# Products without a use of their results in the first steps of an attention, and scale vectors that are loaded later

## The chip, the cores and the metric
One core of a Trainium2 chip runs the whole program. The metric is the time of one execution on the device, in microseconds; the profile gives its span, from the first to the last instruction, and every instruction inside it.

## What is computed
Four blocks, each with a residual sum and a layer normalisation behind it, on 2 x 1024 tokens of 128 features, all in float32:

```
x = LN(x + attention0(x))     # 8 heads of 16, queries and keys; each head's values have 128 columns
x = LN(x + ffn0(x))           # silu(x W1^T * s1) * (x W2^T * s2), then two gelu layers of 512, then back to 128
x = LN(x + attention1(x))     # gated delta rule in chunks of 32, short and long filters
x = LN(x + ffn1(x))           # +1/-1 weights, three layers
```

Attention0, where the change lies, is `softmax((xn Wq + bq)(xn Wk + bk)^T / 4) (xn Wv + bv)` for each of 2 x 8 = 16 heads, and the results are summed over groups of eight. The vectors w1_s, w2_s, h1_s, h2_s (512 numbers each) and w3_s (128) scale the outputs of ffn0's layers.

## The kernel before, in words
The five engines have one program each, and semaphores connect them. The attention is a list of steps written out by hand, `for step in range(LAST + 1)` in the TensorE program. A head is two units of 512 query rows; unit u has four steps. In a step TensorE (PE) does up to four things, for four different stages of the pipeline:

- `scores(u, m)` (line 1629): two products of 50 x 128 by 50 x 512 into a ring of three PSUM banks (4, 5, 6). ScalarE (ACT) turns each into probabilities (line 628, exponential). It lies in step `4(u+1) + 7 + m`.
- `row_scores` (lines 1608, 1609): two products of 48 x 128 by 48 x 512, side by side in the array, into bank pair 0-1 or 2-3. VectorE (DVE) takes the maximum of each row from them (line 1110). Step s needs the maximum of step s - 2 to be taken.
- `shift_to_rows(u)` (line 1617), in step `4(u+1) + 2`: GpSimd (POOL) has split the maxima (lines 803, 804), PE transposes them, ACT copies them (line 622), and the queue of SyncE (SP) sends them by two small DMAs into rows 48 to 49 and 112 to 113 of the query stack (`load_shift`, line 381). `scores(u, 0)` waits for them.
- `pv` (line 1644): 16 products of 128 x 32 by 128 x 128, probabilities times values, into bank 7.

The SP queue is one list in program order. For each head h it has: `load_shift(2h)`, some stores or loads, the stacks of head h + 3 (`load_stacks`, lines 375 and 376, four DMAs of 192 KB, which for h + 3 >= 4 wait until the scores of head h - 1 are done), `load_shift(2h + 1)`, and more stores or loads. Among them, at h = 2, lie the five small loads of the scale vectors (lines 399 and 400), then the weights of ffn0, at h = 7 and 8 the weights of attention1. Steps 1 to 3 also hold the last projections: `project_q(3)`, `project_k(3)`, `project_v(3)`; DVE reads the last of them from bank 7 in `values(3)` (line 1087), behind the maximum of step 4.

ACT and DVE wait for all ffn0 loads, scales and weights together, before ffn0's first silu; POOL waits for them at unit 13, where it begins to split the weights. The scales count in the same semaphore, `w_in`, as the weights.

The names of the diff: `T_BANK[3]` is bank 4, `PVB` bank 7, `MAXB` bank 0; `ksp[0]` and `qsp[0]` hold the split keys and queries of the first 512 tokens and stay unchanged through the attention. `score_step(1, 0)` is step 15, `pv_step(0, 0)` is step 14.

Of the kernel before, what the change touches and what calls it, by code (L numbers as in the profile page):

```python
# [9 lines left out]
P = 128  # L10
# [4 lines left out]
GROUPS = B * S // GT  # L15
# [41 lines left out]
def program(nc, dr, out_dram, x_dram, q_scratch, k_scratch, ctx):  # L57
# [3 lines left out]
    def sem(name):  # L61
        return ctx.enter_context(nc.semaphore(name))

    ps = ctx.enter_context(nc.psum_tensor("ps", [P, 8, 512], F32))
# [23 lines left out]
    def sbw(name, shape, dt=F32):  # L88
        return ffn_weights.enter_context(nc.sbuf_tensor(name, shape, dt))

    W1, W2, WH1, WH2, W3 = 0, FH, 2 * FH, 2 * FH + FB * FH, 2 * FH + 2 * FB * FH
    WCOLS = W3 + FB * D
    w_raw = sbw("w_raw", [P, WCOLS])
    w_hi, w_lo = sbw("w_hi", [P, WCOLS], F32R), sbw("w_lo", [P, WCOLS], F32R)
    ffn_scale = sbw("ffn_scale", [P, 4, FB])
    w3s = sbw("w3s", [P, 1])
    w_in, w_split = sem("ffn_w_in"), sem("ffn_w_split")
    W_LOADS, WSPLITS = 16, WCOLS // 512

    sub = ExitStack()  # L100

# [9 lines left out]
    MAXB, RINGB, PVB = 0, 4, 7  # L111
# [7 lines left out]
    qsp = [qsp_first[:, 0], qsp_first[:, 1], qsp_last[:, 0], qsp_last[:, 1]]  # L119
    ksp = [ksp_first[:, 0], ksp_first[:, 1], ksp_last[:, 0], ksp_last[:, 1]]  # L120
# [119 lines left out]
    with nc.Block() as block:  # L240
        first_sems = []

        def sem_first(name):
            first_sems.append(sem(name))
            return first_sems[-1]
# [9 lines left out]
        q_hi, k_hi, q_lo, k_lo, v_ready = sem_first("q_hi"), sem_first("k_hi"), sem_first("q_lo"), sem_first("k_lo"), sem_first("v_ready")  # L255
# [3 lines left out]
        max_psum, max_done = sem_first("max_psum"), sem_first("max_done")  # L259
# [6 lines left out]
        T_BANK, V_BANK = (4, 5, 4, 4), 7  # L266
# [4 lines left out]
        def score_step(u, m):  # L271
            return 4 * (u + 1) + LAG + m

        def pv_step(u, m):
            return score_step(u, m) + PV_LAG + (u % 2 == 0 and m == 0)

        def shift_step(u):
            return 4 * (u + 1) + 2
# [64 lines left out]
        def _(sp):  # L343
# [4 lines left out]
            def store_q(g, rows, done):  # L348
                b, cols = g // 2, slice(GT * (g % 2), GT * (g % 2) + GT)
                sp.wait_ge(q_lo, g + 1)  # L350
                sp.dma_start(q_scratch[b, rows, 0:2, cols], qsp[g][rows].bitcast(F32)).then_inc(done, 16)
                sp.dma_start(q_scratch[b, rows, 2:3, cols], qsp[g][rows, 0:1].bitcast(F32)).then_inc(done, 16)

            def store_k(g, rows, done):
                b, cols = g // 2, slice(GT * (g % 2), GT * (g % 2) + GT)
                sp.wait_ge(k_lo, g + 1)
                sp.dma_start(k_scratch[b, rows, 1:3, cols], ksp[g][rows].bitcast(F32)).then_inc(done, 16)
                sp.dma_start(k_scratch[b, rows, 0:1, cols], ksp[g][rows, 0:1].bitcast(F32)).then_inc(done, 16)
# [19 lines left out]
            def load_shift(u):  # L378
                sp.wait_ge(ring_done, ring["shift", u] + 1)
                for r in (48, 112):  # L380
                    sp.dma_start(half_of(qst[r:r + 2, (u // 2) % STACKS, :], u % 2).bitcast(F32), shift_sb[:, u % 2, :].bitcast(F32)).then_inc(shift_in[u % 2], 16)
# [12 lines left out]
            store_rows(0, other_rows, splits_stored[0])  # L394
            store_rows(1, other_rows, splits_stored[1])
            def load_ffn_weights(i):
                if i == 0:
                    for j, name in enumerate(("w1", "w2", "h1", "h2")):
                        sp.dma_start(ffn_scale[:, j, :], dr[f"L0_ffn_{name}_s"]).then_inc(w_in, 16)
                    sp.dma_start(w3s[:], dr["L0_ffn_w3_s"].rearrange("(p o) -> p o", o=1)).then_inc(w_in, 16)  # L400
                elif i < 3:
                    o, name = ((W1, "w1"), (W2, "w2"))[i - 1]
                    sp.dma_start(w_raw[:, o:o + FH], dr[f"L0_ffn_{name}_w"]).then_inc(w_in, 16)
                elif i < 11:
                    o, name = ((WH1, "h1"), (WH2, "h2"))[(i - 3) // FB]
                    k = (i - 3) % FB
                    sp.dma_start(w_raw[:, o + FH * k:o + FH * k + FH], dr[f"L0_ffn_{name}_w"][P * k:P * k + P, :]).then_inc(w_in, 16)
                else:
                    sp.dma_start(w_raw[:, W3:W3 + FB * D].rearrange("p (k n) -> p k n", k=FB),
                                 dr["L0_ffn_w3_w"].rearrange("(k p) n -> p k n", p=P)).then_inc(w_in, 16)  # L410

            for h in range(NH):
                load_shift(2 * h)
                if h == 0:
                    load_stacks(2)
                if h in (1, 2):
                    store_k(1 + h, all_rows, splits_stored[1 + h])
                if 2 <= h < 6:
                    load_ffn_weights(3 * h - 6)
                if h + 3 < NH:  # L420
                    load_stacks(h + 3)
                load_shift(2 * h + 1)
                if h in (0, 1):
                    store_q(2 + h, all_rows, splits_stored[2 + h])
                if 2 <= h < 6:
                    load_ffn_weights(3 * h - 5)
                    load_ffn_weights(3 * h - 4)
                if h == 7:
                    for i, n in enumerate(CONVS):
                        sp.dma_start(wqkv[:, i, :], dr[f"L1_attn_W{n}"]).then_inc(w4_in, 16)  # L430
                        sp.dma_start(tap_rows[:, i, :], dr[f"L1_attn_conv_{n}"].rearrange("(o c) k -> o (c k)", o=1).broadcast_to([P, P * CONV])).then_inc(w4_in, 16)
                if h == 8:
                    sp.dma_start(wgates[:, 0:4], dr["L1_attn_Wb"]).then_inc(w4_in, 16)
                    sp.dma_start(wgates[:, 4:8], dr["L1_attn_Wg"]).then_inc(w4_in, 16)
                    sp.dma_start(wgates[:, 8:20], dr["L1_attn_Wl"]).then_inc(w4_in, 16)
                    for dst, name, n in ((gate_bias[:, 0:4], "bg", 4), (gate_bias[:, 4:16], "bl", 12), (temp[:], "log_temp", 4)):
                        sp.dma_start(dst, dr["L1_attn_" + name].rearrange("(o n) -> o n", o=1).broadcast_to([P, n])).then_inc(w4_in, 16)
# [75 lines left out]
        def _(act):  # L513
# [102 lines left out]
            for i, unit in enumerate(ring_order):  # L616
# [6 lines left out]
                else:  # L623
                    _, u, t = unit
                    n = 4 * u + t // 2
# [7 lines left out]
                    if (u, t) == (30, 5):  # L633
                        split_x1(0)

            act.wait_ge(w_in, 16 * W_LOADS)
            silus(0)
            gated_hi(0)
            for g in range(GROUPS):
# [311 lines left out]
        def _(dve):  # L951
# [191 lines left out]
                if step == score_step(30, 3):  # L1143
                    split_x1(0)

            dve.wait_ge(w_in, 16 * W_LOADS)
            gate_up(0, 0)
            gate_up(0, 1)
            for g in range(GROUPS):
# [256 lines left out]
        def _(pe):  # L1406
# [169 lines left out]
            def project_v(g):  # L1576
                if g == 0:
                    pe.wait_ge(wv_summed, 1)
                else:
                    pe.wait_ge(v_ready, g)  # L1580
                for n in range(4):
                    last = nc.tensor.matmul(ps[:, V_BANK, P * n:P * n + P], xnT[:, g % 2, P * n:P * n + P], wv_sum[:], start=True, stop=True)
                last.then_inc(v_psum, 1)
# [48 lines left out]
            def pv(u, m):  # L1632
# [12 lines left out]
                                                start=(t == 0), stop=(t == 7), skip_group_check=True)  # L1645
                last.then_inc(pv_done, 1)

            for step in range(LAST + 1):
                for u in range(UNITS):
                    for m in range(4):  # L1650
                        if score_step(u, m) == step:
                            scores(u, m)
                if step == 0:
                    pe.wait_ge(q_lo, 2)
                    pe.wait_ge(k_lo, 2)
                if step < 4 * UNITS:
                    row_scores(step // 4, step % 4)
                if step == 1:
                    project_q(3)
                if step == 2:  # L1660
                    project_k(3)
                if step == 3:
                    project_v(3)
                if step == shift_step(0):
                    pe.wait_ge(q_lo, GROUPS)
                    pe.wait_ge(k_lo, GROUPS)
                for u in range(UNITS):
                    if shift_step(u) == step:
                        shift_to_rows(u)
                    for m in range(4):  # L1670
                        if pv_step(u, m) == step:
                            pv(u, m)
                if step == 4 * UNITS + 4:
                    pe.wait_ge(max_done, 4 * UNITS)
                    x1_transposes(0)
                if step == score_step(31, 0):
                    pe.wait_ge(w_split, 2 * WSPLITS)
                if score_step(31, 0) <= step <= score_step(31, 3):
                    gate(0, (step - score_step(31, 0),))
# [97 lines left out]
            for b in range(B):  # L1777
# [6 lines left out]
                for n in range(8):  # L1784
                    for h in range(4):
                        for c in range(4):
# [3 lines left out]
                                                    start=True, stop=True)  # L1790
# [43 lines left out]
            for j in range(1, STEPS):  # L1834
                n, c = j // 4, j % 4
                pe.wait_ge(state_ready, j)
                for b in range(B):
                    for h in range(4):
                        f = slice(32 * h, 32 * h + 32)
# [118 lines left out]
```

## Time and profile before

| what | us |
|---|---|
| time, median of 3 runs | 643.23 (640.03 to 653.44) |
| time of the profiled execution | 645.64 |
| its span | 643.9 |
| attention steps, from the first row scores to the last probabilities times values | about 28 to 233 |
| PE busy in the span | 550.5 (85%) |
| DVE busy | 401.0 (62%) |
| ACT busy | 309.8 (48%) |
| POOL busy | 176.0 (27%) |

The profiled execution lies 2.4 us above the median of the runs. "Granted clock" is the clock of TensorE that the chip granted, as a share of 2.4 GHz: 1.00 is 2.4 GHz, 0.50 is 1.2 GHz. Matmuls are pipelined: the duration that the trace gives for one is longer than the distance at which the next one starts.

### The profile page before, as it was taken

How to read it: one execution, taken by the hardware profiler on the slowest of the kernel's cores; microseconds unless marked ns; L12 is line 12 of the kernel's file. 1: busy time of each engine (PE TensorE's matmuls, PEld its weight loads, DVE VectorE, ACT ScalarE, POOL GpSimd, SP SyncE). 2: the span in 40 equal slices, each digit the busy share in tenths (PEclk: the TensorE clock that was granted, in tenths of full speed). 3: DMA queues.
4: the chain of work that ended last, by engine and by line, in shares of the span. 5: the costliest groups of instructions: out<-in, count | busy, mean ns of one | idle time of the engine just before them, and what ended most of it. 6: DMA issues, size and time to landing. Idle time of an engine off the chain costs nothing.

```text
span 643.9 us, 19295 instructions
## 1 busy us (share of the span) xinstructions
PE 550.5 (85%) x8402; PEld 379.3 (59%) x8402; DVE 401.0 (62%) x769; ACT 309.8 (48%) x563; POOL 176.0 (27%) x332
## 2 busy tenths in 40 slices
PE   4779999999999999899898998979984655687994
PEld 2444555555555557777676776755764644465772
DVE  5794779899999834252535345458995303467674
ACT  3224668788888875546464545640042020124431
POOL 7000111344535420010000033249896300010201
PEclk9765889999999999999999999997996565559998
DMA  3886456555250000010000000023033000000011
GB/s 110 184 205 183 123 131 146 107 115 101 53 101 4 5 2 1 0 35 0 1 1 2 0 1 1 9 61 69 4 68 69 4 5 4 6 1 1 0 34 33
DMA packets 37450, 31.83 MB, mean 49 GB/s; under 512 B 22245, under 2 KB 28901, under 8 KB 37366
## 3 DMA queue, kind: packets, MB, share of 16 engines
q1 hardware_dynamic: 36374, 30.08, 20.6%
q8 instruction: 66, 1.08, 0.7%
q10 hardware_dynamic: 992, 0.53, 0.4%
q14 instruction: 18, 0.15, 0.1%
HBM read 20.83 MB, written 9.44 MB: 47 GB/s over the span
## 4 chain that ended last, share of the span: by engine, by line
PE 68%; DVE 11%; ACT 7%; DMA 6%; issue 5%; SPq 1%; POOL 1%; POOLq 0%; DVEq 0%; ACTq 0%
PE ps L1644 10%; PE ps L1629 9%; PE ps L1410 6%; PE ps L1732 6%; PE ps L1411 6%; PE ps L1412 6%; DMA qst<-shift_sb 4%; PE ps L1608 3%; PE ps L1760 2%; PE ps L1891 2%; PE ps L1892 2%; PE ps L1840 2%; PE ps L1788 2%; DVE nmx L1110 2%; DVE hf L978 1%
## 5 line engine op out<-in xcount | busy, mean ns | idle before, releaser
L1110 DVE TENSOR_REDUCE nmx<-ps 128x1 f32<-128x1024 f32 x128 | 154.2, 1218 | 27.0 <-PE ps L1609 25.8
L628 ACT ACTIVATE prob<-ps 128x512 f32<-128x512 f32 x256 | 137.2, 597 | 34.8 <-PE ps L1629 34.0
L1629 PE MATMUL ps<-qst,kst 50*128 50x512 f32 x256 | 78.5, 523 | 7.2 <-DMA qst<-shift_sb 3.9
L1644 PE MATMUL ps<-prob,vp 128*32 128x128 f32 x2048 | 84.2, 292 | 0.0
L1644 PEld LDWEIGHTS ps<-prob,vp 128*32 128x32 f32 x2048 | 52.2, 114 | 42.8 <-ACT prob L628 20.8
L983 DVE TENSOR_TENSOR h_lo<-hf,h_hi 128x512 fp32r<-128x512 f32 x48 | 33.2, 691 | 58.0 <-ACT h_hi L537 57.5
L1608 PE MATMUL ps<-kst,qst 48*128 48x512 f32 x128 | 58.0, 454 | 4.6 <-DVE nmx L1110 4.0
L1410 PE MATMUL ps<-h_hi,w_lo 128*128 128x512 f32 x144 | 59.0, 410 | 2.5 <-DVE h_lo L983 2.1
L1411 PE MATMUL ps<-h_lo,w_hi 128*128 128x512 f32 x144 | 56.9, 395 | 0.0
L1412 PE MATMUL ps<-h_hi,w_hi 128*128 128x512 f32 x144 | 56.8, 394 | 0.0
L1609 PE MATMUL ps<-kst,qst 48*128 48x512 f32 x128 | 56.3, 441 | 0.0
L1629 PEld LDWEIGHTS ps<-qst,kst 50*128 50x128 f32 x256 | 31.7, 195 | 38.7 <-ACT prob L628 24.1
L536 ACT ACTIVATE hf<-ps,ffn_scale 128x512 f32<-128x512 f32 x32 | 22.1, 690 | 45.2 <-PE ps L1412 45.2
L1732 PE MATMUL ps<-vpad,fir_diag 32*32 32x512 f32 x1088 | 38.3, 639 | 0.7 <-issue 0.7
L764 POOL TENSOR_SCALAR rs<-mv 128x4 f32<-128x4 f32 x8 | 2.0, 245 | 131.3 <-DVE mv L961 131.2
L803 POOL CAST nsplit<-nmx 128x4 fp32r<-128x4 f32 x32 | 6.0, 186 | 116.1 <-DVE nmx L1110 113.8
L1410 PEld LDWEIGHTS ps<-h_hi,w_lo 128*128 128x128 f32 x144 | 27.0, 188 | 14.7 <-DVE h_lo L983 9.1
L941 POOL TENSOR_SCALAR rs<-mv 128x4 f32<-128x4 f32 x8 | 1.8, 230 | 118.1 <-DVE mv L1296 118.1
L1732 PEld LDWEIGHTS ps<-vpad,fir_diag 32*32 32x32 f32 x1088 | 26.4, 106 | 12.2 <-issue 5.5
L1608 PEld LDWEIGHTS ps<-kst,qst 48*128 48x128 f32 x128 | 26.1, 205 | 9.2 <-DVE nmx L1110 7.5
L1320 DVE SCALAR_TENSOR_TENSOR h_lo<-ps,h_hi 128x512 fp32r<-128x512 f32 x32 | 21.2, 685 | 16.4 <-ACT h_hi L719 16.4
L1412 PEld LDWEIGHTS ps<-h_hi,w_hi 128*128 128x128 f32 x144 | 27.0, 188 | 6.6
(235 smaller groups left out, 1086.6 us busy)
## 6 DMA issues: line engine op xcount, KB each, us to landing
qst<-q_scratch SPq DMA_DIRECT2D x31, 192.0 KB, 4.6
kst<-k_scratch SPq DMA_DIRECT2D x31, 192.0 KB, 5.0
w_raw<-L_ffn_h_w SPq DMA_DIRECT2D x8, 256.0 KB, 3.9
X<-L_attn_x SPq DMA_DIRECT2D x4, 256.0 KB, 5.2
qst<-shift_sb SPq DMA_DIRECT2D x64, 4.0 KB
q_scratch<-w_hi SPq DMA_DIRECT2D x2, 512.0 KB, 5.6
k_scratch<-w_lo SPq DMA_DIRECT2D x2, 512.0 KB, 3.1
low_dram<-low SPq DMA_DIRECT2D x8, 128.0 KB, 3.0
```

The source lines that it names most:

```text
L536: nc.scalar.activation(hf[:, o, :], bank, ACT.Gelu, scale=scale)
L628: nc.scalar.activation(prob[:, n % PROBS, GT * (t % 2):GT * (t % 2) + GT], ps[:, RINGB + i % RING, :], ACT.Exp, scale=SCORE_SCALE).then_in ...
L983: nc.vector.tensor_tensor(h2_lo[:, layer, o, :], hf[:, o, :], h2_hi[:, layer, o, :].bitcast(F32), ALU.subtract).then_inc(lo2_ready, 1)
L1110: nc.vector.tensor_reduce(nmx[:, u % 2, j:j + 1], pair, AX.X, ALU.max, negate=True).then_inc(max_done, 1)
L1410: nc.tensor.matmul(out, wl, xh, start=start, stop=False)
L1411: nc.tensor.matmul(out, wh, xl, start=False, stop=False)
L1412: return nc.tensor.matmul(out, wh, xh, start=False, stop=stop)
L1608: nc.tensor.matmul(ps[:, bank, :], qst[0:48, p, P * k:P * k + P], kst[0:48, p, 0:GT], start=True, stop=True)
L1609: nc.tensor.matmul(ps[:, bank + 1, :], qst[64:112, p, P * k:P * k + P], kst[64:112, p, GT:S], start=True, stop=True).then_inc(max_psum, 1)
L1629: nc.tensor.matmul(ps[:, RINGB + i % RING, :], kst[r:r + 50, p, P * t:P * t + P], half_of(qst[r:r + 50, p, :], u % 2), start=True, stop=Tr ...
L1644: last = nc.tensor.matmul(ps[32 * j:32 * j + 32, PVB, P * half:P * half + P], vp[:, h, t, :], prob[:, n % PROBS, c:c + P], start=(t == 0), ...
L1732: last = nc.tensor.matmul(ps[32 * g:32 * g + 32, 4 * k + h, :], fir_diag[f, (0, FIRL)[k] + t, :], vpad[f, g // 2, off:off + GT], start=(t ...
```

## The change
TensorE gets a helper, `fill(bank, n)`: n products of 128 x 128 by 128 x 512 from `ksp[0]` and `qsp[0]`, whose result is overwritten by the next use of the bank and read by nobody. They stand in steps 2 to 5 (two each, bank 4), in steps 6 to 13 (two each, bank 7) and in step 15 ahead of `scores(1, 0)` (six, bank 2): 30 in all. Step 6 gets a wait for `v_ready`, that DVE has read the last values out of bank 7, ahead of its two products; step 15 gets a wait for `max_done` of 14, the one that its row scores have anyway, ahead of its six.

The five loads of the scale vectors move in the SP queue from h = 2, between `load_shift(4)` with the store of keys and `load_stacks(5)`, to h = 9, behind `load_shift(19)`. They count in a semaphore of their own, `scales_in`. ACT and DVE wait for that one at ffn0's start, and POOL for the eleven weight loads alone.

```diff
-    w_in, w_split = sem("ffn_w_in"), sem("ffn_w_split")
-    W_LOADS, WSPLITS = 16, WCOLS // 512
+    w_in, w_split, scales_in = sem("ffn_w_in"), sem("ffn_w_split"), sem("ffn_scales_in")
+    W_LOADS, SCALES, WSPLITS = 11, 5, WCOLS // 512
...
             def load_ffn_weights(i):
-                if i == 0:
-                    for j, name in enumerate(("w1", "w2", "h1", "h2")):
-                        sp.dma_start(ffn_scale[:, j, :], dr[f"L0_ffn_{name}_s"]).then_inc(w_in, 16)
-                    sp.dma_start(w3s[:], dr["L0_ffn_w3_s"].rearrange("(p o) -> p o", o=1)).then_inc(w_in, 16)
-                elif i < 3:
+                if i < 3:
...
-                if 2 <= h < 6:
+                if 3 <= h < 6:
                     load_ffn_weights(3 * h - 6)
...
+                if h == 9:
+                    for j, name in enumerate(("w1", "w2", "h1", "h2")):
+                        sp.dma_start(ffn_scale[:, j, :], dr[f"L0_ffn_{name}_s"]).then_inc(scales_in, 16)
+                    sp.dma_start(w3s[:], dr["L0_ffn_w3_s"].rearrange("(p o) -> p o", o=1)).then_inc(scales_in, 16)
...
-            act.wait_ge(w_in, 16 * W_LOADS)
+            act.wait_ge(scales_in, 16 * SCALES)
...
-            dve.wait_ge(w_in, 16 * W_LOADS)
+            dve.wait_ge(scales_in, 16 * SCALES)
...
+            def fill(bank, n):
+                for _ in range(n):
+                    nc.tensor.matmul(ps[:, bank, :], ksp[0][:, 0, 0:P], qsp[0][:, 0, :], start=True, stop=True)
+
             for step in range(LAST + 1):
+                if step == score_step(1, 0):
+                    pe.wait_ge(max_done, step - 1)
+                    fill(MAXB + 2 * (step % 2), 6)
...
                 if step == 3:
                     project_v(3)
+                if 2 <= step < 6:
+                    fill(T_BANK[3], 2)
+                if step == 6:
+                    pe.wait_ge(v_ready, GROUPS)
+                if 6 <= step < pv_step(0, 0):
+                    fill(PVB, 2)
```

## Rows read from the trace of the kernel before

**Rows 1.** Page: granted clock and DMA share in 40 slices; chain by engine

```profile
PEclk9765889999999999999999999997996565559998
DMA  3886456555250000010000000023033000000011
...
PE 68%; DVE 11%; ACT 7%; DMA 6%; issue 5%; SPq 1%; POOL 1%; POOLq 0%; DVEq 0%; ACTq 0%
```

**Rows 2.** Windows: PE, PEld, DVE, ACT, POOL busy (instructions), clock, DMA share, GB/s

```profile
26.00:36.00 10.00, 7.25 (x37) 3.83 (x35) 8.26 (x9) 2.73 (x4) 0.39 (x2) 1.00 1.04 296
36.10:50.60 14.50, 11.50 (x61) 6.06 (x61) 12.15 (x12) 4.82 (x11) 0.77 (x4) 0.50 0.79 159
50.70:70.00 19.30, 19.30 (x170) 10.03 (x174) 10.37 (x11) 9.54 (x19) 1.62 (x6) 0.50 0.47 137
...
84.00:87.00 3.00, 3.00 (x38) 1.55 (x30) 2.08 (x2) 1.81 (x4) 0.32 (x2) 0.50 0.04 14
...
94.30:128.00 33.70, 32.41 (x487) 17.94 (x486) 30.57 (x31) 27.16 (x55) 7.53 (x22) 1.00 0.59 122
...
268.00:275.00 7.00, 5.25 (x24) 3.76 (x22) 4.02 (x7) 2.92 (x5) 0.00 (x0) 1.00 0.00 0
```

**Rows 3.** Timeline of PE, steps 6 to 15: start, us, line, operation, count, idle before

```profile
36.94 0.38 PE L1617 MATMUL ps<-ident,nsplit 128*8 128x128 f32 x1
...
41.33 0.79 PE L1608 MATMUL ps<-kst,qst 48*128 48x512 f32 x1 [0.34 <-DVE nmx L1110]
...
47.10 1.94 PE L1644 MATMUL ps<-prob,vp 128*32 128x128 f32 x32
...
50.66 0.79 PE L1629 MATMUL ps<-qst,kst 50*128 50x512 f32 x2 [1.32 <-DMA qst<-shift_sb]
```

**Rows 4.** Chain that ended last, at steps 4 and 15: start, us, what

```profile
36.16 0.60 DVE vp L1087
...
43.41 7.21 DMA qst<-shift_sb
```

**Rows 5.** Timeline of DVE: maxima of steps 5 to 11

```profile
36.67 8.18 DVE L1110 TENSOR_REDUCE nmx<-ps 128x1 f32<-128x1024 f32 x7
```

**Rows 6.** Timeline of ACT: the first eight exponentials

```profile
43.19 4.05 ACT L628 ACTIVATE prob<-ps 128x512 f32<-128x512 f32 x8 [0.47 <-PE ps L1629]
```

**Rows 7.** Timeline of PE: first scores of units 2 and 7

```profile
59.61 0.79 PE L1629 MATMUL ps<-qst,kst 50*128 50x512 f32 x2
...
94.30 0.50 PE L1629 MATMUL ps<-qst,kst 50*128 50x512 f32 x2
```

**Rows 8.** Timeline of PE: first scores of unit 13

```profile
128.06 0.50 PE L1629 MATMUL ps<-qst,kst 50*128 50x512 f32 x2 [0.17 <-DMA qst<-shift_sb]
```

**Rows 9.** Timeline of PE in ffn0, at clock 1.00

```profile
268.65 0.39 PE L1412 MATMUL ps<-h_hi,w_hi 128*128 128x512 f32 x1
268.88 0.39 PE L1410 MATMUL ps<-xt_hi,w_lo 128*128 128x512 f32 x1
...
272.63 0.50 PE L1410 MATMUL ps<-xt_hi,w_lo 128*128 128x512 f32 x1 [1.75 <-DVE X L988]
```

**Rows 10.** Timeline of PE in ffn1, at clock 0.50

```profile
576.07 0.63 PE L1879 MATMUL ps<-x_lo,sw 128*128 128x512 f32 x1
576.50 0.63 PE L1880 MATMUL ps<-x_lo,sw 128*128 128x512 f32 x1
```

**Rows 11.** Timeline of PE: first scores of unit 5

```profile
81.86 0.50 PE L1629 MATMUL ps<-qst,kst 50*128 50x512 f32 x2 [1.50 <-DMA qst<-shift_sb]
```

**Rows 12.** Timeline of the SP queue, head 2

```profile
71.38 2.03 SPq L399 DMA_DIRECT2D ffn_scale<-L_ffn_w_s  x2
...
74.41 0.43 SPq L400 DMA_DIRECT2D w3s<-L_ffn_w_s  x1
74.88 0.43 SPq L375 DMA_DIRECT2D qst<-q_scratch  x1
```

**Rows 13.** Timeline of the SP queue, last load of head 8, shift of unit 18

```profile
150.24 0.43 SPq L437 DMA_DIRECT2D temp<-L_attn_log_temp  x1
150.81 1.27 SPq L381 DMA_DIRECT2D qst<-shift_sb  x2
```

## The prediction, made before the change was run

> **What bounds the kernel now.** I read the page's 40 slices first, then a table of windows over the first 130 us, then PE's timeline with the idle time of each row, and last the chain and the SP queue. The slices show a granted clock of 0.5 to 0.8 between about 16 and 100 us, under a chain that is 68% PE [rows 1]: where PE is the bound, its clock is the price of the step. The windows say where the clock goes [rows 2]. It is 1.00 from 26 to 36 us, 0.50 from 36.1 to 70, then 1.00, with one more dip at 84 to 87, and 1.00 through the rest of the attention. Two stretches of half clock differ in kind:
>
> - 36.1 to 50.6 us (steps 6 to 14). PE is busy 11.50 of 14.50 us, but the work goes at DVE's pace: seven maxima in 8.18 us, 1.17 each [rows 5], and then at ACT's, eight exponentials in 4.05 us [rows 6]. The row scores of step 10 still wait 0.34 us for DVE at half clock [rows 3]. Then PE waits 1.32 us for the shift of unit 1, whose DMAs take 7.21 us behind 1.5 MB of stacks [rows 3, 4]. A faster clock buys next to nothing here, since that DMA decides.
> - 50.7 to 70 us. PE is busy 19.30 of 19.30 us, DVE 10.37, ACT 9.54 [rows 2]. PE alone is the bound, at 1.2 GHz. Unit 1 takes from 50.66 to 59.61, 8.95 us [rows 3, 7]; six units at full clock take 94.30 to 128.06, 5.63 us each [rows 7, 8].
>
> So the loss that the change can reach is this: steps 15 to 38 take 94.30 - 50.66 = 43.64 us, and the next 24 steps, of the same work and with the same kind of shift waits, 33.76 us [rows 3, 7, 8]. The difference is 9.88 us. The rest of the span isn't touched by any edit.
>
> **The change part by part.** *The 30 products themselves.* Their form is that of ffn0's: at full clock one follows another by 268.88 - 268.65 = 0.23 us, at half clock by 576.50 - 576.07 = 0.43 us [rows 9, 10]. That is 6.9 us or 12.9 us of PE, so they need cover.
>
> - Steps 2 to 5, two each (0.46 us at full clock). These steps are DVE's: in 26 to 36 us PE has 2.75 us idle, DVE 1.74 [rows 2], and most of DVE's own idle lies ahead of step 2. Nothing waits for PE longer than a maximum. Cost 0; without the cover, 4 x 0.46 = 1.8 us.
> - Steps 6 to 13, two each. A step is row scores (0.23 us at full clock, by the spacing of one 512-column product) and 0.46 us more, 0.7 us against 1.17 us of DVE: hidden. In steps 11 to 13 the two scores add 0.46 us: 1.15 us against DVE's 1.17 us. Just hidden. At half clock the same steps are 1.3 us (6 to 10), and about 1.05 + 0.86 = 1.9 us (11 to 13), no longer hidden.
> - The wait at step 6. Behind it stand the products, the transpose of shift 0 and the row scores of step 7. `values(3)` ends at 36.16 + 0.60 = 36.76 [rows 4], the transpose ran at 36.94 [rows 3]. Now it starts at about 36.76 + 0.46 = 37.2: 0.3 us later. SP's queue hands this on (shift 0, eight stack loads, shift 1), and the shift of unit 1 is the path, so I book +0.3 us; the bounds are 0 and, at half clock, +0.7 us.
> - The six at step 15. Their wait costs nothing: maximum 13 is long taken, since DVE was ahead of it. At full clock the 32 products of `pv` take about half of 1.94 us [rows 3], so PE comes to step 15 near 48.2 instead of 49.35, runs 6 x 0.23 = 1.4 us, is done at 49.6, and the shift lands at 50.7 to 51.0. Hidden, with an idle rest of 1.1 to 1.4 us.
>
> *What they may do to the clock.* No row shows these products in these steps; the bounds are no effect (0) and the whole 9.88 us. For an effect: the clock went to 0.50 at 36 us after stretches in which PE had little but row scores, and in ffn0 an idle of 1.75 us, with dense 128 x 128 x 512 products on both sides, left it at 1.00 [rows 2, 9]. With the products PE is at work over half of each step from 2 to 14, with the whole array. Even if the clock falls at 36 us, steps 6 to 10 at half clock would be filled by these products, of the form at which ffn0 keeps 1.00. I take 9.88 us as the likeliest, and take off 0.7 us: the stores of the third and fourth query and key groups (768 KB each) fall into these heads and not into the later three, and at the quicker pace they lie closer to the shifts. Bounds of this term: 0 and 2.5 us (four odd shifts later by 0.6).
>
> The page "TensorE: Matmul & The Clock Gate" of the Trainium skill (Part 1) says that the clock's throttle is released when PE is busy and comes back when it idles. This trace does not agree for 50.7 to 70 us: PE was busy 19.30 of 19.30 us at 0.50 [rows 2]. By the page's rule the old kernel should have been at full clock soon after 51 us, and there would be little to win.
>
> *The scales.* At h = 2 they hold the SP queue from 71.38 to 74.84, 3.46 us, and `load_stacks(5)` starts at 74.88, with shift 5 behind it [rows 12]; PE then waited 1.50 us for that shift [rows 11], and the second dip of the clock (84 to 87) followed [rows 2]. At the full clock four steps last 5.6 us, and shift 4 (1.3 us), the key store (0.9) and the scales (3.46) fill them; without the scales SP is free 1 us ahead. This gain is inside the 33.76 us, whose heads have no scales at that place. At h = 9 they stand behind `load_shift(19)` and ahead of `load_shift(20)`, four steps later. Head 8 shows the price: six small loads in that place end at 150.67 and shift 18 goes out at 150.81, on time [rows 13]; 3.46 us fit where 3.8 did. Cost 0, bounds 0 and 0.3 us. The waits at ffn0's start are met some 70 us before. POOL's wait for eleven loads is no longer.
>
> **Sum.** -9.88 + 0.3 + 0.7 = -8.9 us. Against the profiled execution 645.64 - 8.9 = 636.7; that execution is 2.4 us above the median, so the median goes from 643.23 to 634.3.
>
> **The rivals.**
>
> - *The clock is won and lost again at step 15.* PE still idles 1.1 to 1.4 us there for the shift, perhaps 1.9 if `pv` comes earlier. At 81.86 an idle of 1.50 us was followed by the dip [rows 2, 11]. Against it: the 1.75 us in ffn0 [rows 9], and the six dense products just ahead. The price is the time at half clock: between the 3 us of the dip and the 19 us after 50.7, each costing 1 - 5.63 / 8.95 = 37% of itself, so 1.1 to 7 us of the gain, 4 in the middle: 638.3 us.
> - *The clock doesn't answer* (the change doesn't do what it says). Hidden fills, clock 0.50 until about 70 us as before; only the scales' part stays, about 1 us: 642 us. For it: busy PE at half clock for 19 us [rows 2].
> - *Slower: the fills run at half clock and lie on the path, at step 15.* Steps 6 to 10 cost 5 x (1.29 - 1.17) = 0.6 us, steps 11 to 13 3 x 0.86 = 2.6 us, the six products 6 x 0.43 = 2.6 us: 5.8 us, less the 1.32 us that PE waited [rows 3], +4.5 us, and the clock still comes only at 70 us. 643.23 + 4.5 = 647.7 us. It decides when the clock is at 0.50 from 36 us until beyond step 15. Against it: 5 us of full-array work at 100% should lift it sooner than the old mixture did.
> - *More than forecast.* Other executions of before may lose the clock longer than the profiled one (one took 653.44), and the products guard against it: 630 us or less.
>
> **How the numbers follow.** Forecast 0.50, won and lost 0.22, no answer 0.10, slower 0.08, more than forecast 0.10. The predicted time is the forecast's, 634.3 us. The range reaches to the lost-again case and the no-answer case above and, for the scatter between runs (the lowest of before is 3.2 us under its median), to 630 below: 630 to 644.5. That leaves out the slower case and half of the last. A difference of 2%, 12.9 us, is about what a measurement of this kernel can tell from no change; all of the mechanism is 9.88 us, so faster by over 2% needs the last case and some of the scatter: 0.12. Slower by over 2% has no mechanism that reaches 656: 0.03. Within 2%: 0.85.
>
> **What would show it right or wrong.** Granted clock 1.00 from 26 us through 100; first scores of unit 1 at about 51.0 with a wait of 1 to 1.5 us for the shift DMA; first scores of unit 7 at about 85.4 instead of 94.30; transpose of shift 0 near 37.2; the wait of unit 5 for its shift under 1 us; shift 20 issued right behind its copy; no wait of ACT or DVE for scales. A clock of 0.50 after 53 us says the first rival, at 37 to 50 us with scores of unit 1 beyond 53 us the slower one. The prediction would also be wrong if the clock of a later stage (430 to 580 us, at 0.5 to 0.9 [rows 1]) falls otherwise after the shift in time.

## The result and the profile after

The changed kernel takes 635.95 us (median of 4, 635.23 to 637.1), the kernel before 643.26 us beside it: a ratio of 0.9892, with an interval of 0.9846 to 0.9937. Medians here and below are of all executions; the ratios leave out those that took over 1.5% longer than the fastest of the same kernel. The change makes the kernel faster by 1.1%: the whole interval lies below 1, and the gain is less than 2%. The profiled execution took 636.29 us, 9.35 us less than the profiled execution before; its span is 634.5 us.

The page of the changed kernel, granted clock and DMA share in 40 slices, and the chain by engine:

```profile
PEclk9799999999999999999999999978986655568998
DMA  3778675554320000010000000213033000000011
...
PE 67%; DVE 11%; DMA 7%; ACT 7%; issue 5%; SPq 1%; POOL 1%; POOLq 0%; DVEq 0%; ACTq 0%
```

The third to the sixth slice (about 32 to 95 us) are at 9, where [rows 1] had 6, 5, 8, 8. The windows of the changed kernel over the same stretches (columns as in rows 2; the last two run from the first scores of unit 7 to those of unit 13, and over the end of PE's wait in attention1 and the start of its filters):

```profile
26.00:36.00 10.00, 9.20 (x45) 5.02 (x43) 8.06 (x9) 2.73 (x4) 0.39 (x2) 1.00 1.02 278
36.10:50.60 14.50, 13.31 (x84) 6.57 (x83) 12.44 (x12) 5.11 (x11) 0.77 (x4) 1.00 0.76 166
50.70:70.00 19.30, 18.85 (x285) 10.53 (x287) 16.97 (x16) 15.60 (x31) 2.41 (x10) 1.00 0.75 217
...
84.20:117.60 33.40, 32.45 (x488) 17.99 (x488) 30.21 (x31) 26.97 (x54) 7.57 (x22) 1.00 0.57 125
420.00:431.00 11.00, 8.07 (x228) 4.55 (x229) 8.40 (x17) 2.21 (x4) 9.90 (x15) 0.58 0.24 37
```

Against [rows 2] the clock is 1.00 in 36 to 70 us, and in 50.7 to 70 us PE does 285 products instead of 170, with DVE busy 16.97 us instead of 10.37. The timeline of PE in the changed kernel, with the added products on line 1650:

```profile
30.96 1.03 PE L1650 MATMUL ps<-qsp,ksp 128*128 128x512 f32 x2
...
37.01 0.73 PE L1650 MATMUL ps<-qsp,ksp 128*128 128x512 f32 x2
37.57 0.27 PE L1617 MATMUL ps<-ident,nsplit 128*8 128x128 f32 x1
...
44.12 0.51 PE L1629 MATMUL ps<-qst,kst 50*128 50x512 f32 x2
...
45.45 0.50 PE L1629 MATMUL ps<-qst,kst 50*128 50x512 f32 x2
...
48.48 1.63 PE L1650 MATMUL ps<-qsp,ksp 128*128 128x512 f32 x6
50.94 0.50 PE L1629 MATMUL ps<-qst,kst 50*128 50x512 f32 x2 [0.83 <-DMA qst<-shift_sb]
...
72.81 0.50 PE L1629 MATMUL ps<-qst,kst 50*128 50x512 f32 x2
...
84.23 0.51 PE L1629 MATMUL ps<-qst,kst 50*128 50x512 f32 x2 [0.40 <-DMA qst<-shift_sb]
```

The first two products, those of step 2, start at 30.96. Shift 0 is transposed at 37.57 instead of 36.94 [rows 3]. The six products end at 50.11 and PE waits 0.83 us more for the shift; the scores of unit 1 start at 50.94, 0.28 us later than before. Unit 5 (72.81) has no wait where [rows 11] had 1.50 us. Unit 7 starts at 84.23 instead of 94.30 [rows 7], 10.07 us earlier. The SP queue at head 9, the place of the scales now:

```profile
145.99 1.27 SPq L381 DMA_DIRECT2D qst<-shift_sb  x2
147.31 0.99 SPq L430 DMA_DIRECT2D ffn_scale<-L_ffn_w_s  x2
148.34 0.91 SPq L430 DMA_DIRECT2D ffn_scale<-L_ffn_h_s  x2
149.29 0.43 SPq L431 DMA_DIRECT2D w3s<-L_ffn_w_s  x1
151.26 1.28 SPq L381 DMA_DIRECT2D qst<-shift_sb  x2
```

The queue is empty at 149.72 and shift 20 goes out 1.5 us later, when it is ready: nothing is paid there. The first silu of ffn0 starts 10.3 us earlier (224.9 for 235.2), and the filters too (425.94 for 436.20). Behind them 0.9 us is given back: from the first filter product to the end of the span it takes 208.6 us instead of 207.7, in stages where the clock moves between 0.5 and 1.0 in both kernels.

### The profile page after: what moved, and what is told of

It reads as the page before. It is cut to its first block, busy times and chain, and to the rows that moved or that the text cites. A ratio compares the mean times of both kernels' runs of the same rounds, so it can differ in the third digit from the quotient of the medians.

```text
span 634.5 us, 19355 instructions
## 1 busy us (share of the span) xinstructions
PE 546.9 (86%) x8432; PEld 379.9 (60%) x8432; DVE 399.9 (63%) x769; ACT 310.0 (49%) x563; POOL 175.9 (28%) x332
## 4 chain that ended last, share of the span: by engine, by line
PE 67%; DVE 11%; DMA 7%; ACT 7%; issue 5%; SPq 1%; POOL 1%; POOLq 0%; DVEq 0%; ACTq 0%
PE ps L1644 9%; PE ps L1629 8%; PE ps L1410 6%; PE ps L1745 6%; PE ps L1412 6%; PE ps L1411 6%; DMA qst<-shift_sb 5%; PE ps L1608 2%; PE ps L1773 2%; PE ps L1904 2%; PE ps L1905 2%; PE ps L1853 2%; PE ps L1801 2%; ACT prob L628 2%; DVE hf L978 2%
## 5 line engine op out<-in xcount | busy, mean ns | idle before, releaser
L1644 PE MATMUL ps<-prob,vp 128*32 128x128 f32 x2048 | 78.9, 278 | 0.0
L1629 PE MATMUL ps<-qst,kst 50*128 50x512 f32 x256 | 73.6, 492 | 5.5 <-ACT prob L628 3.4
L1644 PEld LDWEIGHTS ps<-prob,vp 128*32 128x32 f32 x2048 | 49.1, 109 | 39.7 <-ACT prob L628 22.4
L1608 PE MATMUL ps<-kst,qst 48*128 48x512 f32 x128 | 52.7, 413 | 1.4 <-DMA kst<-k_scratch 0.8
L1609 PE MATMUL ps<-kst,qst 48*128 48x512 f32 x128 | 51.4, 403 | 0.0
L1629 PEld LDWEIGHTS ps<-qst,kst 50*128 50x128 f32 x256 | 29.3, 183 | 35.8 <-ACT prob L628 22.9
L1745 PEld LDWEIGHTS ps<-vpad,fir_diag 32*32 32x32 f32 x1088 | 29.1, 107 | 9.1 <-issue 4.2
L1411 PEld LDWEIGHTS ps<-h_lo,w_hi 128*128 128x128 f32 x144 | 27.1, 188 | 5.5
```

Source lines behind the costliest of these rows:

```text
L1411: nc.tensor.matmul(out, wh, xl, start=False, stop=False)
L1608: nc.tensor.matmul(ps[:, bank, :], qst[0:48, p, P * k:P * k + P], kst[0:48, p, 0:GT], start=True, stop=True)
L1609: nc.tensor.matmul(ps[:, bank + 1, :], qst[64:112, p, P * k:P * k + P], kst[64:112, p, GT:S], start=True, stop=True).then_inc(max_psum, 1)
L1629: nc.tensor.matmul(ps[:, RINGB + i % RING, :], kst[r:r + 50, p, P * t:P * t + P], half_of(qst[r:r + 50, p, :], u % 2), start=True, stop=Tr ...
L1644: last = nc.tensor.matmul(ps[32 * j:32 * j + 32, PVB, P * half:P * half + P], vp[:, h, t, :], prob[:, n % PROBS, c:c + P], start=(t == 0), ...
L1745: last = nc.tensor.matmul(ps[32 * g:32 * g + 32, 4 * k + h, :], fir_diag[f, (0, FIRL)[k] + t, :], vpad[f, g // 2, off:off + GT], start=(t ...
```

## The experiments

Theory: products in the gaps of steps 2 to 13 hold the clock, and nearly all of the gain is theirs; the scales are worth about 1 us. Rivals: the scales' place is the cause; the time at half clock isn't fixed by the kernel at all; the six products of step 15 are what counts.

The marks of all profiles, in us (start of the first scores of a unit; "3 to 13" is the time from unit 3 to unit 13; "mean clock" is the granted clock over the whole span, lowest to highest of the executions in the ratio):

| kernel | median | ratio to before, interval | clock 0.50, in 27 to 100 us | unit 1 | unit 3 | wait of unit 5 | 3 to 13 | mean clock |
|---|---|---|---|---|---|---|---|---|
| before | 643.26 | | 36 to 70, 84 to 87 | 50.66 | 68.73 | 1.50 | 59.33 | 0.882 to 0.909 |
| before, again | 643.57 (one) | | 36 to 50, 74 to 98 | 49.12 | 60.55 | 1.89 | 66.35 | 0.884 (one) |
| the change | 635.95 | 0.9892 (0.9846 to 0.9937) | none | 50.94 | 61.87 | 0 | 55.69 | 0.911 to 0.918 |
| products alone | 640.96 | 0.9951 (0.9895 to 1.0007) | 74 to 80 | 50.50 | 61.44 | 1.69 | 59.64 | 0.907 to 0.918 |
| scales alone | 636.48 | 0.9911 (0.9859 to 0.9964) | 36 to 56 | 50.16 | 63.81 | 0 | 55.13 | 0.892 to 0.903 |
| scales alone, again | 637.68 | 0.9948 (0.9859 to 1.0036) | 38 to 59 | 50.28 | 64.66 | 0.27 | 55.25 | 0.889 to 0.907 |
| without 2 to 5 | 642.38 | 0.9998 (0.9963 to 1.0033) | 29 to 56 | 58.16 | 69.17 | 0 | 55.55 | 0.898 to 0.908 |
| without the six | 635.62 | 0.9898 (0.9839 to 0.9957) | 51 to 58 | 49.92 | 63.49 | 0 | 55.30 | 0.914 to 0.919 |
| only the six | 637.10 | 0.9935 (0.9882 to 0.9987) | 37 to 51 | 51.36 | 62.28 | 0.23 | 55.28 | 0.899 to 0.907 |
| transposes | 640.03 | 0.9965 (0.9928 to 1.0001) | none | 55.18 | 66.11 | 0 | 55.06 | 0.911 to 0.922 |
| one each | 638.01 | 0.9870 (0.9776 to 0.9963) | 36 to 53 | 54.68 | 65.67 | 0 | 55.47 | 0.900 to 0.910 |
| shift 1 first | 635.02 | 0.9834 (0.9760 to 0.9908) | none | 49.19 | 60.12 | 0 | 55.60 | 0.910 to 0.919 |
| 15 before the triangles | 632.70 | 0.9808 (0.9730 to 0.9887) | none | 50.38 | 61.34 | 0 | 55.27 | 0.918 to 0.921 |
| both | 633.44 | 0.9801 (0.9713 to 0.9890) | none | 49.86 | 61.12 | 0 | 55.35 | 0.920 to 0.922 |

The kernel before had a median of 645.59 us beside products alone, scales alone, without 2 to 5 and without the six (the mean clock of its row is of those executions), 648.16 beside the repetitions, only the six and transposes, and 646.50 beside the last four.

**Products alone.** The five scale loads stay in head 2 and in `w_in`:

```diff
-                if i < 3:
+                if i == 0:
+                    for j, name in enumerate(("w1", "w2", "h1", "h2")):
+                        sp.dma_start(ffn_scale[:, j, :], dr[f"L0_ffn_{name}_s"]).then_inc(w_in, 16)
...
+                elif i < 3:
```

> The 30 products, with the scale loads left where the kernel before has them. If the products hold the clock and that is the gain: granted clock 1.00 from 26 to 75 us, first scores of unit 3 near 62 us as after the change, but a wait of unit 5 for its shift that is about 1 us longer (1.5 us or more, none after the change), perhaps a dip of the clock behind it; time 636 to 638.5 us. If the gain came from the scales' place in the SP queue: little of it here, 641 us or more.

640.96 us, between the two forecasts, with a ratio (0.9951) that isn't clear of 1. The clock stays at 1.00 up to the wait of unit 5, and falls there. PE's timeline and the SP queue of this kernel:

```profile
72.18 0.27 PE L1617 MATMUL ps<-ident,nsplit 128*8 128x128 f32 x1
74.15 0.80 PE L1629 MATMUL ps<-qst,kst 50*128 50x512 f32 x2 [1.69 <-DMA qst<-shift_sb]
```

```profile
64.12 1.52 SPq L399 DMA_DIRECT2D ffn_scale<-L_ffn_w_s  x2
...
66.66 0.43 SPq L400 DMA_DIRECT2D w3s<-L_ffn_w_s  x1
67.14 0.43 SPq L375 DMA_DIRECT2D qst<-q_scratch  x1
```

The stacks of head 5 start at 67.14, right behind the scales, and at 66.16 in the changed kernel: 1 us, as worked out (1.4 us measured from unit 3, which starts 0.43 us earlier here). But the wait brings 6.8 us at 1.2 GHz with it, and unit 7 starts at 87.92 instead of 84.23: 3.7 us. By the prediction's 37% the half clock costs 2.5 us of it, an estimate, and the wait, less the lead of 0.43 us, the rest.

**Scales alone.** The changed kernel without `fill` and its calls:

```diff
-                if 2 <= step < 6:
-                    fill(T_BANK[3], 2)
...
-                if 6 <= step < pv_step(0, 0):
-                    fill(PVB, 2)
```

> The scale loads moved, none of the products. If the products hold the clock: clock 0.50 from 36 to about 70 us as before, no dip at 84 us since the wait of unit 5 is about 1 us shorter; time 641 to 643 us. If the scales' place is the cause of the gain: 637 us or less.

636.48 us: the rival's number, not the theory's. The clock fell at 36 us as before, but returned at 56, while the first step that differs from the kernel before comes behind 62 us. So either the return is chance, or the profile misled. Two repetitions ask that.

> The kernel before once more, for a second profile of it. If the return of the clock at 70 us is fixed by the work: it falls at about 36 us and returns at about 70 us again, scores of unit 2 at 59.6 us and of unit 7 at 94.3 us. If the return is a matter of chance, as the scales alone (return at 56 us, before any moved load is reached) suggest: another time of return, between 56 and 90 us, and the dip behind the wait of unit 5 for its shift in some profiles only.

> The scale loads alone once more. If the early return of the clock (56 us) was chance: another time of return here, and a median of more than the first 636.5 us. If it comes with the kernel: 56 us and 636.5 us again. In both cases no wait of unit 5 above 1 us and no half clock after 80 us.

The windows of the kernel before, in its second profile:

```profile
37.00:49.00 12.00, 10.38 (x58) 5.69 (x58) 10.92 (x10) 4.40 (x10) 0.78 (x4) 0.50 0.82 173
50.00:73.00 23.00, 20.98 (x322) 11.66 (x320) 20.27 (x20) 18.00 (x36) 3.29 (x12) 1.00 0.73 186
74.00:97.00 23.00, 23.00 (x210) 11.81 (x210) 12.88 (x13) 11.78 (x24) 2.02 (x8) 0.50 0.36 83
```

and PE's timeline between the last two:

```profile
71.28 0.27 PE L1617 MATMUL ps<-ident,nsplit 128*8 128x128 f32 x1
73.44 0.63 PE L1629 MATMUL ps<-qst,kst 50*128 50x512 f32 x2 [1.89 <-DMA qst<-shift_sb]
```

The same kernel, the same clock fall at 36 us, and then the other way round: back at 50 us instead of 70, but 24 us of half clock instead of 3 behind unit 5's wait. By unit 13 both profiles stand alike, at 128.06 and 126.90. Four profiles (before twice, scales alone twice) run the same program up to 62 us; the clock returned in them at 70, 50, 56 and 59 us. That is chance as far as the kernel goes. What isn't is the part behind unit 3: "3 to 13" is 59.33 to 66.35 us in the three profiles with the scales in head 2, all with a wait of 1.5 us or more and a fall of the clock, and 55.06 to 55.69 us in all eleven without them there, in none of which the clock falls between 60 and 230 us.

The mean clocks show the same for the products, over all executions in the ratios and not in one profile: 0.911 to 0.918 in the changed kernel, 0.889 to 0.907 in both runs of the scales alone. The products do hold the clock. But the times of these kernels, 635.95 for 636.48 and 637.68 us, differ by no more than their scatter.

**Without 2 to 5, and without the six.** One of the two places is taken out of the changed kernel each time:

```diff
-                if 2 <= step < 6:
-                    fill(T_BANK[3], 2)
```

> The changed kernel without the eight products of steps 2 to 5. If the clock of the attention's units 1 to 6 needs only dense work shortly before step 15: the clock falls to 0.50 at 36 us, comes back between 39 and 47 us under the products of steps 6 to 13, and the time is within 1 us of the changed kernel's 636. If it must never fall at 36 us: 0.50 until about 70 us, and 645 us or more, with steps 11 to 15 longer by 4 to 5 us.

```diff
-                if step == score_step(1, 0):
-                    pe.wait_ge(max_done, step - 1)
-                    fill(MAXB + 2 * (step % 2), 6)
```

> The changed kernel without the six products of step 15. PE then idles about 2.3 us there for the shift of unit 1. If these six guard the clock: it falls to 0.50 within 4 us after step 15 and stays there for 3 to 19 us, time 637.5 to 643 us. If the products of steps 2 to 13 suffice: clock 1.00 throughout and the same 636 us.

Without steps 2 to 5 the clock falls at 29.1 us in the profile. That fall isn't the missing products' doing: they would have started at about 31 us, and PE had waited 2.57 us just before, ahead of the first row scores. In the five profiles of kernels that have the same program up to step 6 (before, scales alone, only the six) it falls at 36 to 38 us. What the run does show is what happens when the products of steps 6 to 13 meet a low clock: the theory's hope that they bring it back at once fails. The windows and PE's timeline of this kernel:

```profile
30.00:56.00 26.00, 25.10 (x86) 11.89 (x88) 18.47 (x17) 5.64 (x12) 1.17 (x6) 0.50 0.67 184
57.00:100.00 43.00, 42.34 (x618) 23.39 (x616) 37.95 (x37) 34.34 (x69) 5.70 (x22) 1.00 0.67 167
```

```profile
27.53 0.46 PE L1608 MATMUL ps<-kst,qst 48*128 48x512 f32 x1 [2.57 <-DMA kst<-k_scratch]
...
49.01 0.79 PE L1629 MATMUL ps<-qst,kst 50*128 50x512 f32 x2
...
51.31 0.79 PE L1629 MATMUL ps<-qst,kst 50*128 50x512 f32 x2
...
56.60 1.63 PE L1650 MATMUL ps<-qsp,ksp 128*128 128x512 f32 x6
58.16 0.50 PE L1629 MATMUL ps<-qst,kst 50*128 50x512 f32 x2
```

PE is busy 25.10 of 26 us at 0.50. A step of 11 to 13 takes 2.30 us, and unit 1 starts at 58.16, 7.2 us later than in the changed kernel. This is the slower rival of the prediction, alive: products that meet a low clock lie on the path. The kernel is no faster than before (0.9998), and the mean clock of all ten executions (0.898 to 0.908) is under that of the changed kernel, so the low clock isn't a matter of the one profile.

Without the six, PE idles 2.04 us, the clock falls at 51.1 and is back at 57.9:

```profile
49.92 0.50 PE L1629 MATMUL ps<-qst,kst 50*128 50x512 f32 x2 [2.04 <-DMA qst<-shift_sb]
```

```profile
52.00:57.00 5.00, 5.00 (x50) 2.51 (x52) 2.67 (x3) 2.83 (x6) 0.37 (x2) 0.50 0.15 53
```

Unit 3 is 1.6 us later, yet the time is that of the changed kernel (635.62), not the 637.5 to 643 us expected for that case. In this profile the clock fell without the six as expected, but they are worth no more than a run's scatter.

**Only the six.** Steps 2 to 13 without products.

> The changed kernel with the six products of step 15 alone. The clock falls at 36 us as before, and the six run at half clock: 2.6 us, of which the wait for the shift covers 1.3. If products guard only a clock that is high: no return before 55 us, scores of unit 1 at about 52 us, time 637 to 643 us. If the six dense products bring the clock back: 1.00 from about 53 us, unit 7 at about 86 us, 637 us or less.

```profile
48.74 2.69 PE L1650 MATMUL ps<-qsp,ksp 128*128 128x512 f32 x6
51.36 0.50 PE L1629 MATMUL ps<-qst,kst 50*128 50x512 f32 x2
```

The six run at half clock, 2.69 us, and the clock is back at 51.1 us, while they run. Unit 1 starts 0.4 us behind the changed kernel and unit 13 at the same 117.56. The profiled execution took 634.3 us, the median is 637.10, with mean clocks of 0.899 to 0.907: both as with the scales alone (636.48 and 637.68 us, 0.889 to 0.907). So no gain of the six by themselves is shown. One profile can't say that they caused the return, since it came at 50 us without them in the second profile of before.

**Transposes.**

```diff
-                    nc.tensor.matmul(ps[:, bank, :], ksp[0][:, 0, 0:P], qsp[0][:, 0, :], start=True, stop=True)
+                    for c in range(4):
+                        nc.tensor.transpose(ps[:, bank, P * c:P * c + P], xn[:, 0, c, :], ident[:])
```

> The changed kernel with four transposes of 128 x 128 in the place of each product, the same 512 columns. If the clock asks for products and not for a busy PE (the Trainium skill, page TensorE: Matmul & The Clock Gate, Part 4, says that transposes don't count as busy): clock 0.50 from 36 us, the transposes on the path from step 6 to 15, 642 us or more. If any busy PE does: 1.00 throughout, 636 to 638 us.

Windows of this kernel:

```profile
27.00:50.00 23.00, 22.02 (x146) 14.91 (x145) 18.98 (x19) 5.22 (x11) 1.16 (x6) 1.00 0.77 193
50.00:100.00 50.00, 49.03 (x728) 28.71 (x730) 42.85 (x43) 38.39 (x78) 6.53 (x24) 1.00 0.70 175
```

The clock holds at 1.00 with transposes as well. Eight of them take 1.0 us where two products take 0.5, steps 11 to 13 become 1.69 us, the 24 of step 15 take 2.7, and unit 1 starts at 55.18: 4.2 us later, and the time is 4.1 us longer (640.03). A fill that is longer than the gap costs what it is longer by.

**One each.** One product in the place of two in steps 2 to 13.

> The changed kernel with one product instead of two in each of steps 2 to 13; the six stay. If any work of PE in the gaps holds the clock and half of it is enough: 1.00 throughout, scores of unit 1 up to 0.7 us earlier, 635 to 636.5 us. If the amount counts: the clock falls between 30 and 48 us, as without steps 2 to 5, or later; 636 to 642 us.

638.01 us. The clock falls at 36.4 us, where it falls without any products too, and the rest is on the path at half clock; unit 1 starts at 54.68. In the seven profiles with two products, or eight transposes, in each of steps 2 to 5 the clock is at 1.00 until step 15 or longer; in the seven with one or none it falls between 29 and 38 us.

**Two more edits.** The shift of unit 1 goes out ahead of the stacks of head 3:

```diff
+                if h == 0:
+                    load_shift(1)
                 if h + 3 < NH:
                     load_stacks(h + 3)
-                load_shift(2 * h + 1)
+                if h:
+                    load_shift(2 * h + 1)
```

> The changed kernel with the shift of unit 1 sent ahead of the stacks of head 3 in the SP queue. If that shift's DMA sets the start of step 15: it goes out at about 42.9 us instead of 44.4, lands before 50 us, scores of unit 1 start at about 50.1 us, when the six products end, 0.8 us earlier than after the change; all later marks and the time follow, 635 us. If something else is as late (stacks of head 3, the exponentials): no gain.

And 15 products stand in another gap with a fallen clock behind it, PE's wait of 4.12 us ahead of the last triangle products of attention1, where bank 1 is free:

```diff
             v_to_tokens(GROUPS - 1)
+            for _ in range(15):
+                nc.tensor.matmul(ps[:, 1, :], wc_hi[:, 0, 0, :], wc_lo[:, 0].rearrange("p k c -> p (k c)"), start=True, stop=True)
             triangles(GROUPS - 1)
```

> The changed kernel with 15 more products, in PE's wait of 4.1 us at 418 to 422 us, into a bank that is free. If the clock falls there for want of work: 1.00 from 420 to 440 us instead of 0.50 for some 5 to 10 us, filters done 1 to 3 us earlier from their start, 633.5 to 635.5 us. If the filters' 32 x 32 products lower the clock anyway, or their pace isn't PE's clock: no gain, 636 us or up to 1 us more.

> Both of the last two edits on the changed kernel: the sum of what they gain alone, 632.5 to 635 us if both do, below 635 and with a narrow spread.

The first one sends the shift at 42.29 us, unit 1 starts at 49.19 with no wait, 1.75 us before the changed kernel's, and unit 13 is 1.84 us earlier. That is the better of two pairs of profiles: between the second edit alone and both edits, which differ by the same move, it is 50.38 and 49.86 for unit 1, 116.61 and 116.47 for unit 13. The second holds the clock where it falls to 0.50 in the changed kernel (0.58 on the mean over 420 to 431 us above). The changed kernel's PE, then this kernel's:

```profile
422.21 1.96 PE L1542 MATMUL ps<-kq 32*32 32x64 f32 x128 [4.12 <-DVE kq L1007]
```

```profile
416.41 3.68 PE L1736 MATMUL ps<-wc_lo,wc_hi 128*128 128x512 f32 x15
420.79 1.48 PE L1542 MATMUL ps<-kq 32*32 32x64 f32 x128 [0.70 <-DVE kq L1007]
```

```profile
424.00:459.00 35.00, 35.00 (x1091) 24.42 (x1060) 29.71 (x50) 2.25 (x5) 31.39 (x48) 1.00 0.16 34
```

Its filters take 34.3 us from the first to the last (423.5 to 457.8) instead of 37.0, and the triangles' stage 0.9 us less; of this, 2.1 us is given back behind the filters (173.7 us to the end of the span instead of 171.6). It is the fastest version by median, 632.70 us; both edits together gave 633.44, with a ratio of 0.9801. Both are faster than the kernel before by their intervals, which leave open whether by more than 2%. The changed kernel's 635.95 us and these times weren't measured side by side, so 3 us between them is likely and not shown by an interval; that the two edits add up isn't shown.

## Why the prediction was right, and where not

- **Result.** 634.3 us was forecast, 635.95 came, inside 630 to 644.5, with a verdict of within 2%, which had 0.85. Against the sum of -8.9 us the medians moved by 7.3 us and the profiled executions by 9.35. The sum was read from an execution that lay 2.4 us above its median, and was then taken off the median; the second profile of before (643.57) is 7.3 us above the changed kernel's. And it took its 9.88 us whole from a stretch in which both edits work, so it came out although the split between them was wrong. That part of the hit is luck.
- **The clock of steps 15 to 38** was the term of 9.88 us, less 0.7. Between the marks of unit 1 and unit 7 the changed kernel needs 84.23 - 50.94 = 33.29 us, for 43.64 before: 10.35 us. The allowance of 0.7 us for the stores wasn't needed. The mechanism held: at 1.00 these steps are as long as the later ones.
- **But the term wasn't a property of the kernel.** I read one profile, and gave its 9.88 us to the products. Unit 3 starts at 68.73, 60.55, 63.81 and 64.66 us in the four profiles without products, 64.4 on average, for 61.87 with them: 2.6 us is what the products bring up to there, not 7. Where the clock happens to return at 50 us they cost 1.3. Two more profiles with all thirty products (products alone, 15 before the triangles) have 61.44 and 61.34 us.
- **The scales** were priced at "about 1 us", the length of SP's queue. The queue part was right (66.16 for 67.14). The step that failed is that a longer wait costs only itself: the wait of 1.5 to 1.9 us was followed by half clock for 3, 7 and 24 us in the three profiles that have it. From unit 3 to 13 the move is worth 59.64 - 55.69 = 3.9 us beside the products, and 4.2 and 11.1 us without them. Hence the second rival (the clock doesn't answer, and only the scales' part stays, 642 us) was mis-sized too: scales alone gave 636.48 and 637.68. At unit 7 the two edits can be set against each other: 94.30 and 91.35 us with neither, 87.92 with the products alone, 85.85 and 86.89 with the scales alone, 84.23 with both. The scales' move is the larger part by these marks in either order, and the surer one; I had it the other way round. In total time the difference is weaker: the products alone aren't clear of the kernel before (0.9951), the scales alone are in one of two runs (0.9911 and 0.9948), and on top of the scales' move the products bring 0.5 to 1.7 us of median, within the scatter.
- **The products' own cost.** Steps 2 to 10 hide them, as worked out. Steps 11 to 13 were worked out at 1.15 us and took 45.45 - 44.12 = 1.33, so PE is the bound in them; before they took 1.05. That is 0.8 us, and only the late shift covers it. When the shift is sent earlier, unit 1 still starts as soon as the six end. The transpose came 0.63 us later in the pair of profiles, for 0.3 worked out, and unit 1 0.28 us later. But without products the transpose lies between 36.39 and 37.15 us in five profiles, so one pair can't check a term of 0.3.
- **Step 15.** 0.83 us of idle was left, for 1.1 to 1.4 expected; the clock held, and the first rival (won and lost at step 15) didn't come in this profile. Without the six it did.
- **If the clock falls all the same.** The prediction had steps 6 to 10 then "filled by these products, of the form at which ffn0 keeps 1.00", and against the slower rival that such work "should lift it sooner than the old mixture did". Neither held. In the run without steps 2 to 5 the same products ran from 37.6 to 53.7 us at 0.50, the clock came back at 56 us, within the 50 to 70 of the old mixture, and unit 1 was 7.2 us later than in the changed kernel and 7.5 later than before. The slower rival was real at this mark, larger than its 4.5 us. One product per step in place of two met it as well (unit 1 at 54.68).

## What to carry to other kernels

A wait in front of TensorE can cost more than its length where TensorE is the bound behind it, as the 1.5 to 1.9 us ahead of unit 5 did: first shorten the wait (here by moving five tiny loads out of a queue), then think of filling it. Products without a use held the clock here, but what they brought beyond the shorter wait is within the scatter of the times; longer than the gap, or met by a clock that is already low, they lay on the path and cost 4 to 7 us. A loss of clock seen in one profile can sit elsewhere in the next: take a second profile of the same kernel before giving it to a cause.

## What was not expected of the hardware

- A TensorE that the trace counts as all but fully busy stayed at 1.2 GHz for 19 us and more. The granted clock was 0.50 with PE busy 19.30 of 19.30 us [rows 2], 23.00 of 23.00 in the second profile of before, and 25.10 of 26 us with 128 x 128 x 512 products in it. Part 1 of "TensorE: Matmul & The Clock Gate" of the Trainium skill, by which activity releases the throttle, isn't borne out in these stretches. What did bring the clock back isn't settled: in the four profiles without products it came at 50, 56, 59 and 70 us, in the same kind of work.
- With idles of 1.50, 1.69, 1.89 and 2.04 us between attention steps the clock fell to 0.50, in one case during the idle and in three up to 2.0 us behind it; with 0.85, 0.83 and 0.40 us it didn't. Length alone doesn't decide: 1.78 us ahead of the first row scores (scales alone, again) left it at 1.00 for another 10 us, and the 1.75 us in ffn0 [rows 9] didn't lower it either.
- The same page says in Part 4 that the full clock doesn't engage for transposes, which wouldn't count as a busy PE. Here it held at 1.00 from 27 to 100 us with 120 transposes in the place of the 30 products, though real products stood between them.
